# Two-layer cross-attention on one Trainium2 core: the row maxima split on ScalarE and TensorE instead of VectorE, and one 512-column value product per key group

## What is computed

```python
def layer(hidden, context, mask, Wq, bq, Wk, bk, Wv, bv, Wo, bo, gamma, beta):
    q = (hidden @ Wq + bq)      # 8 key groups x 4 heads x 128 x 8
    k, v = context @ Wk + bk, context @ Wv + bv
    scores = einsum('bkgld,bksd->bkgls', q, k) / sqrt(8) + mask
    attn = softmax(scores, axis=-1)
    out = einsum('bkgls,bksd->bkgld', attn, v) @ Wo + bo
    x = out + hidden
    return (x - mean(x)) * rsqrt(var(x) + 1e-6) * gamma + beta
```

## Time and profile before

| | us |
|---|---|
| median of three runs | 337.89 |
| the profiled execution | 340.19 |
| its span on the core | 338.3 |
| TensorE matmul busy | 292.6 (86%) |
| VectorE busy | 271.5 (80%) |
| ScalarE busy | 209.1 (62%) |
| GpSimd busy | 194.0 (57%) |

### The profile page before, as it was taken

The page is one execution under the profiler, slowest core; times in us unless marked ns, Lnnn a source line. Parts: engine busy times, 40 slices in busy tenths (PEclk is TensorE's granted clock), DMA queues, the critical chain, the costliest instruction groups (busy, mean ns, idle before and its releaser), DMA issues.

```text
span 338.3 us, 8301 instructions
## 1 busy us (share of the span) xinstructions
PE 292.6 (86%) x2890; PEld 196.8 (58%) x2890; DVE 271.5 (80%) x625; ACT 209.1 (62%) x500; POOL 194.0 (57%) x335
## 2 busy tenths in 40 slices
PE   7466399599998999999899999999999999888851
PEld 4366276277666776776566666666666666554320
DVE  4426449489988998999899999999999999999441
ACT  3601257277766777777677777777777777656540
POOL 6123305366766776776656666666666666444464
PEclk9756769699999999999999999999999999999795
DMA  7584766714674446344634434444444444420000
GB/s 280 168 237 114 213 182 179 212 31 122 182 242 135 118 124 183 100 125 131 178 101 112 115 109 120 126 121 137 132 119 121 137 141 130 122 64 18 20 16 31
DMA packets 34555, 44.40 MB, mean 131 GB/s; under 512 B 11857, under 2 KB 28241, under 8 KB 31697
## 3 DMA queue, kind: packets, MB, share of 16 engines
q1 hardware_dynamic: 33952, 43.27, 44.7%
q10 hardware_dynamic: 560, 0.59, 0.5%
HBM read 33.10 MB, written 9.96 MB: 127 GB/s over the span
## 4 chain that ended last, share of the span: by engine, by line
PE 37%; DVE 35%; DMA 14%; issue 9%; SPq 2%; ACT 1%; POOL 1%; POOLq 0%; ACTq 0%; DVEq 0%
DVE row_max L460 18%; DMA q_stack<-max_parts 9%; PE misc_bank L663 8%; PE s_bank L567 7%; PE t_bank L587 7%; PE oT_bank L647 7%; DVE o_sb L481 4%; DMA q_scratch<-q_parts 4%; PE qkv_bank L613 3%; DVE z L499 3%; DVE attnT L492 3%; DVE max_parts L468 2%; DVE recip L487 2%; PE qkv_bank L619 2%; PE qkv_bank L623 1%
## 5 line engine op out<-in xcount | busy, mean ns | idle before, releaser
L460 DVE TENSOR_REDUCE row_max<-s_bank 128x4 f32<-128x512 f32 x256 | 168.8, 678 | 35.9 <-PE s_bank L567 35.0
L365 ACT ACTIVATE probs<-t_bank 128x512 f32<-128x512 f32 x256 | 148.0, 601 | 77.8 <-PE t_bank L587 77.4
L587 PE MATMUL t_bank<-q_stack,k_stack 75*128 75x512 bf16 x256 | 99.8, 393 | 20.4 <-DMA q_stack<-max_parts 12.6
L567 PE MATMUL s_bank<-k_stack,q_stack 72*128 72x128 bf16 x1024 | 102.3, 225 | 8.2 <-DMA k_stack<-k_scratch 7.4
L567 PEld LDWEIGHTS s_bank<-k_stack,q_stack 72*128 72x128 bf16 x1024 | 76.2, 101 | 53.1 <-issue 18.5
L307 POOL TENSOR_TENSOR rstd<-var_eps,minus_half 128x1 f32<-128x1 f32 x32 | 17.6, 548 | 56.0 <-DVE var_eps L507 56.0
L316 POOL TENSOR_TENSOR attn<-o_sb,recip 128x256 f32<-128x256 f32 x32 | 20.0, 625 | 40.0 <-DVE recip L487 39.7
L587 PEld LDWEIGHTS t_bank<-q_stack,k_stack 75*128 75x128 bf16 x256 | 25.0, 99 | 28.4 <-ACT probs L365 13.1
L663 PE MATMUL misc_bank<-wo_sb,attnT 128*128 128x256 f32 x128 | 36.0, 405 | 5.7 <-DVE attnT L492 5.7
L190 POOL TENSOR_TENSOR q_rest<-qT,q_parts 128x256 f32<-128x256 f32 x30 | 20.1, 669 | 34.4 <-ACT q_parts L374 34.4
L374 ACT ACTIVATE qT<-qkv_bank,bq_scaled 128x128 f32<-128x128 f32 x60 | 22.1, 369 | 22.6 <-PE qkv_bank L623 20.8
(11 more groups left out here) (76 smaller groups left out, 359.2 us busy)
## 6 DMA issues: line engine op xcount, KB each, us to landing
q_stack<-q_scratch SPq DMA_DIRECT2D x32, 576.0 KB
q_scratch<-q_parts SPq DMA_DIRECT2D x32, 192.0 KB, 6.2
k_stack<-k_scratch SPq DMA_DIRECT2D x32, 144.0 KB
in_sb<-inputs SPq DMA_DIRECT2D x3, 1024.0 KB, 7.9
x_sb<-x SPq DMA_DIRECT2D x4, 512.0 KB, 5.5
result<-y SPq DMA_DIRECT2D x16, 128.0 KB, 1.7
k_scratch<-k_parts SPq DMA_DIRECT2D x48, 32.0 KB, 3.5
mask_sb<-mask SPq DMA_DIRECT2D x1, 1024.0 KB, 7.2
```

The lines of the kernel that those rows point to most:

```text
L365: nc.scalar.activation(probs[:, u % 2, kv], t_bank[kv % 2][:], ACT.Exp).then_inc(exp_done, 1)
L460: nc.vector.tensor_reduce(row_max[:, u % 2, GROUP * kv:GROUP * (kv + 1)], s_bank[(KV * u + kv) % S_BANKS][:].rearrange("p (g s) -> p g s", ...
L567: mm = nc.tensor.matmul(to[:, g * S:(g + 1) * S], q_stack[0:TERM_ROWS, slot, GROUP * kv + g], k_stack[0:TERM_ROWS, slot, kv], start=(g == ...
L587: mm = nc.tensor.matmul(t_bank[kv % 2][:], k_stack[0:STACK_ROWS, slot, kv], q_stack[0:STACK_ROWS, slot, GROUP * kv:GROUP * (kv + 1)], star ...
```

## The change

The three bf16 parts of the maxima are now made without VectorE. ScalarE copies `maxT_ps` as bf16 (part 0). TensorE then adds minus that part onto `maxT_ps` in place, with a product of a 32 x 32 minus identity and the part's rows. ScalarE copies what is left (part 1), TensorE takes it off as well, and ScalarE copies the rest (part 2). `row_max` is transposed one place earlier in the phase, in front of `scores(t, 1)`. ScalarE's `norm` moves behind the third exponential of the phase. In the value product, the two halves now write the same 512 columns: the first half's weights are [v | ones | 0 | 0], the second's [0 | 0 | v | ones], and the second accumulates on the first. So each key group takes one product of 512 columns. The tiles of values get other places for values and zeros, and the rows of Wo are permuted on the host to match. GpSimd makes the minus identity once.

```diff
-MAXT_STEPS, FLIP_STEPS, NORM_STEPS, LN_STEPS = 3, 3, 4, 4
+MAX_PARTS_STEPS, FLIP_STEPS, NORM_STEPS, LN_STEPS = 3, 3, 4, 4
+VHALF = HALF * VW + 2 * HD
...
+        minus_ident = sb("minus_ident", [2 * HEADS, HEADS], BF16)
...
         (SP) load_max_rows
-                sp.wait_ge(maxT_step, MAXT_STEPS * (u + 1))
+                sp.wait_ge(max_part, MAX_PARTS_STEPS * (u + 1))
...
         (ScalarE)
-            def max_first(u):
-                act.wait_ge(maxT_ready, u + 1)
-                need(act, max_rows_loaded[u % 2], 16 * (u // 2))
-                nc.scalar.activation(max_parts[0:HEADS, u % 2], maxT_ps, ACT.Copy).then_inc(max_high, 1)
+            def max_rows(u, part):
+                act.wait_ge(maxT_ready, MAX_PARTS_STEPS * u + part + 1)
+                if part == 0:
+                    need(act, max_rows_loaded[u % 2], 16 * (u // 2))
+                nc.scalar.activation(max_parts[HEADS * part:HEADS * (part + 1), u % 2], maxT_ps,
+                                     ACT.Copy).then_inc(max_part, 1)
...
                 exp(g)
+                if live(t - 1):
+                    max_rows(t - 1, 0)
+                    max_rows(t - 1, 1)
                 exp(g + 1)
                 if live(t - 1):
-                    max_first(t - 1)
+                    max_rows(t - 1, 2)
+                exp(g + 2)
                 if live(t - 4):
                     norm(t - 4)
-                exp(g + 2)
...
         (VectorE)
-            def max_rows(u):
-                high, mid, low = (max_parts[HEADS * n:HEADS * (n + 1), u % 2] for n in range(PARTS))
-                dve.wait_ge(max_high, u + 1)
-                nc.vector.tensor_tensor(mid, maxT_ps, high, ALU.subtract).then_inc(maxT_step, 1)
-                nc.vector.tensor_tensor(rest_ps, maxT_ps, high, ALU.subtract).then_inc(maxT_step, 1)
-                dve.wait_ge(maxT_step, MAXT_STEPS * u + 2)
-                nc.vector.tensor_tensor(low, rest_ps, mid, ALU.subtract).then_inc(maxT_step, 1)
...
         (TensorE)
-                else:
-                    need(pe, maxT_step, MAXT_STEPS * u)
-                nc.tensor.transpose(maxT_ps, row_max[:, u % 2], identf[:]).then_inc(maxT_ready, 1)
+                need(pe, max_part, MAX_PARTS_STEPS * u)
+                nc.tensor.matmul(maxT_ps, row_max[:, u % 2], identf[:], is_transpose=True,
+                                 start=True, stop=False, skip_group_check=True).then_inc(maxT_ready, 1)
+
+            def take_part(u, part):
+                if u == 0:
+                    pe.wait_ge(minus_step, 3)
+                pe.wait_ge(max_part, MAX_PARTS_STEPS * u + part + 1)
+                rows_of = slice(HEADS * part, HEADS * (part + 1))
+                nc.tensor.matmul(maxT_ps, minus_ident[rows_of], max_parts[rows_of, u % 2],
+                                 start=False, stop=(part == 1), skip_group_check=True).then_inc(maxT_ready, 1)
...
-                for odd in range(2):
-                    for j in range(HALF):
-                        kv = half * HALF + j
-                        first = kv * VW + 2 * HD * (1 - odd)
-                        v = v_ones[:, b % RING, first:first + VW] if layer == 0 else v_later[:, b, first:first + VW]
-                        mm = nc.tensor.matmul(
-                            oT_bank[32 * j:32 * (j + 1), half * 2 * L:(half + 1) * 2 * L].rearrange("p (a l) -> p a l", a=2), v,
-                            probs[:, u % 2, kv].rearrange("p (a c l) -> p c a l", a=2, c=2)[:, odd],
-                            start=(odd == 0), stop=(odd == 1), skip_group_check=True)
+                for j in range(HALF):
+                    first = half * HALF * VW + j * VW
+                    v = v_ones[:, b % RING, first:first + VW] if layer == 0 else v_later[:, b, first:first + VW]
+                    mm = nc.tensor.matmul(oT_bank[VW * j:VW * (j + 1)], v, probs[:, u % 2, half * HALF + j],
+                                          start=(half == 0), stop=(half == 1), skip_group_check=True)
...
                 if live(t - 3):
                     probs_v(t - 3, 1)
+                if live(t - 1):
+                    transpose_max(t - 1)
                 scores(t, 1, masked)
                 scoresT(g + 1, masked)
                 if live(t - 1):
-                    transpose_max(t - 1)
+                    take_part(t - 1, 0)
                 scores(t, 2, masked)
                 scoresT(g + 2, masked)
+                if live(t - 1):
+                    take_part(t - 1, 1)
                 if live(t + AHEAD):
                     project(t + AHEAD)
```

More of the change, by code:

```diff
@@ L100, in cross_attention @@
         max_parts = sb("max_parts", [PARTS * HEADS, 2, L], BF16)
[L101 to L102 removed]
+        v_ones = sb("v_ones", [P, RING, 2 * VHALF], F32)
+        v_later = sb("v_later", [P, BATCH, 2 * VHALF], F32)
         probs = sb("probs", [P, 2, KV, GROUP * L], F32)
@@ L172, in cross_attention @@
         maxT_ready = sem("maxT_ready")
-        max_high = sem("max_high")
-        maxT_step = sem("maxT_step")
+        max_part = sem("max_part")
+        minus_step = sem("minus_step")
         scoresT_ready = sem("scoresT_ready")
@@ L206, in blocks_of @@
         def blocks_of(v):
-            return v[:, :, 0:KV * VW].rearrange("p r (h c) -> p r h c", c=VW)
+            return [v[:, :, h * VHALF:h * VHALF + HALF * VW].rearrange("p r (j c) -> p r j c", c=VW) for h in range(2)]
         block = ctx.enter_context(nc.Block())
@@ L295, in _ @@
             nc.gpsimd.memset(mask_sum[:], 0.0).then_inc(sum_cleared, 1)
+            nc.gpsimd.memset(minus_ident[:], 0.0).then_inc(minus_step, 1)
+            for n in range(2):
+                pool.wait_ge(minus_step, n + 1)
+                nc.gpsimd.affine_select(out=minus_ident[:], in_=minus_ident[:], compare_op=ALU.not_equal, fill=-1.0,
+                                        base=-HEADS * n, pattern=[[-1, HEADS]], channel_multiplier=1).then_inc(minus_step, 1)
             nc.gpsimd.memset(minus_half[:], -0.5).then_inc(consts_set, 1)
@@ L298, in _ @@
             pool.wait_ge(v_later_padded, 1)
-            nc.gpsimd.memset(blocks_of(v_later)[:, :, :, 3 * HD:4 * HD], 1.0).then_inc(v_later_padded, 1)
+            for half in blocks_of(v_later):
+                nc.gpsimd.memset(half[:, :, :, HD:2 * HD], 1.0).then_inc(v_later_padded, 1)
             def deviation(u):
@@ L445, in _ @@
             dve.wait_ge(v_padded, 1)
-            nc.vector.memset(blocks_of(v_ones)[:, :, :, 3 * HD:4 * HD], 1.0).then_inc(v_padded, 1)
+            for half in blocks_of(v_ones):
+                nc.vector.memset(half[:, :, :, HD:2 * HD], 1.0).then_inc(v_padded, 1)
             def flag():
@@ L458, in maximum @@
                 if kv == 0:
-                    need(dve, maxT_ready, u - 1)
+                    need(dve, maxT_ready, MAX_PARTS_STEPS * (u - 2) + 1)
                 nc.vector.tensor_reduce(row_max[:, u % 2, GROUP * kv:GROUP * (kv + 1)],
@@ L748 @@
         "w_kv": by_partition(np.concatenate([w[:, k_order] for w in both("Wk")] + both("Wv"), axis=1)),
-        "w_o": np.concatenate([by_partition(w) for w in both("Wo")], axis=1),
+        "w_o": np.concatenate([by_partition(w[o_order]) for w in both("Wo")], axis=1),
         "rows": np.stack([np.concatenate(r) for r in zip(both("bo"), both("gamma"), both("beta"), both("bv"))]),
```

17 lines of the change are left out of this document (7 added, 10 removed).

## The result

On one chip the changed kernel takes 340.96 us (median of four runs, 340.13 to 343.14) and the kernel before 337.92 (four runs, 336.97 to 338.07): a ratio of 1.0106, 95% interval 1.0055 to 1.0156. The forecast was 333.4 and faster, so it is off by 7.6 us and has the wrong sign. The profiled execution of before took 340.19 us (span 338.3), 2.3 above the median that the forecast stood on. The one of after took 341.09 (span 339.0) and lies at its median. So the spans differ by only 0.7, and the forecast for the span, 333.5, was 5.5 us off.

A forecast was written before the change was run, and what follows sets the result against it. TensorE was taken to bound layer 0 and VectorE layer 1; terms of +3.0, -2.0, +0.3, -0.7, -3.2, -2.2 and 0 summed to -4.8 on the 338.3 span, giving 333.4 us, eight in ten between 327.5 and 341.

The forecast's parts named there:

- What bounds the kernel: Whole kernel: TensorE alone sets layer 0's full phases of 8.74 us, VectorE sets layer 1's of 8.48.
- So going in costs 0.09 and coming out 0.10, and one small product costs 0.06 + 0.19 = 0.25.: TensorE's price for each 32 x 32 product, columns plus changes of shape; two make +0.5 us a phase.
- the forecast +3.0: Six full phases of layer 0, each 0.5 us longer by the two small products.
- So they leave 1.5 earlier ... I take -2.0, as the issue moves by more than any of the waits.: Layer 0's four long phases: rows of maxima issued 1.5 us earlier, the wait of 1.09 nearly vanishing, -2.0 together.
- 0 if the landing does not move: Layer 0's four long phases: alternative outcome with no gain, against -2.8 if the wait goes entirely.
- The projections (0.9 or 1.8 us) cover that for TensorE: Each phase: ScalarE's second exponential comes about 0.5 us later, but TensorE does not wait, being busy with projections.
- the 8.12 of layer 1: Nine phases of layer 1: TensorE's 7.62 + 0.5 in place of 8.48, each -0.36, together -3.2 us.
- in place of 8.34: Five phases from 169.0 us: TensorE's 7.84 + 0.5 = 8.34, each -0.14, together -0.7 us.
- the 2.2: Last three phases before 312.5 us: no projection left, VectorE's 0.83 comes out nearly whole, -2.2 us.
- Rival 1: TensorE stands still at the small products in every phase, +0.3 each over 28 phases: slower, 341.5 us; chance 0.22.
- Rival 3: Layer 1 stays at 8.48 through ScalarE's later exponentials or the output projection: 337.0 us, about no change; chance 0.13.
- The step from span to median: Whole kernel: profiled execution 2.3 us above the median, so span forecast 333.5 became 333.1 on the median, given as 333.4.

The follow-up runs named there:

- the full-array run: Changed kernel with both small products over the whole array (weights 96 x 128, zero outside the part) against the kernel before: 339.61 us, ratio 1.0041.
- the value product: Kernel before with only the new value product, one 512-column product per key group, against the kernel before: 338.86 us against 339.55, ratio 1.0001.
- the moves: Kernel before with only the earlier transposition, ScalarE's copy before the second exponential and norm behind the third, VectorE still splitting: 339.69 us, ratio 1.0037.
- its maxima alone: Changed kernel with the old value product, two 256-column products per key group, against the kernel before: 341.26 us, ratio 1.0022.
- its copy with fewer loads: Changed kernel without layer 1's 16 loads of the keys' rows (144 KB each), against the kernel before: 339.93 us against 339.39, ratio 1.0012.
- one product and one subtraction: Layer 0 as before; layer 1 with one whole-array product, two ScalarE copies and one VectorE subtraction, against the kernel before: 334.69 us against 340.25, ratio 0.9873.
- the run with the first part only: Kernel before without VectorE's three subtractions, parts two and three of the maxima zero, against the kernel before: 335.32 us against 339.87, ratio 0.9876.

## Why the prediction was wrong, step by step

**What bounds the kernel.** Right: TensorE in layer 0, VectorE in layer 1. What was not asked is what stands right behind VectorE. The runs found three limits within 0.3 us below 8.48: TensorE with its two products (8.22), ScalarE's way from the transposition to the fifth exponential (8.33), and the transfers of a phase (8.36 on average without the split). The last is no fixed floor, since the changed kernel ran at an even 8.34 with its rows landing 0.3 to 0.9 us before TensorE needed them.

**"So going in costs 0.09 and coming out 0.10, and one small product costs 0.06 + 0.19 = 0.25."** Right to 0.01, and the full-array run showed that 0.09 of it, on the way out, is the change of shape. The neighbour was left out: the float32 products behind the second one cost 0.10 more. A phase of layer 0 pays 0.60, not 0.50. That the full phases still sum to the forecast +3.0 is luck: five paid 0.6 each, and the sixth, 9.31 at a granted clock of 0.94 before and 9.34 at 1.00 after, paid next to nothing.

**"So they leave 1.5 earlier ... I take -2.0, as the issue moves by more than any of the waits."** The step that failed in layer 0, by 2.1 us. The issue did move, by 1.0 to 1.4 us, but the landing moved by -0.1 to +0.2. The prediction had named this case ("0 if the landing does not move") but put -2.0 of -2.8 on the other. The landing follows the transfers ahead of the rows. That is read from the traces, as no run relieved the transfers of layer 0.

**"The projections (0.9 or 1.8 us) cover that for TensorE"** and the 8.12 of layer 1. The failed step of layer 1, 2.1 us. In the changed kernel a phase has 0.10 more for the projections and 0.11 for the exponential that comes late at the seventh product. The late exponential alone would have been enough, since the run over the whole array took the same 8.33 with 0.2 less on TensorE and a wait of 0.32. The same two stand in the phases from 169 us, where 8.56 was measured in place of 8.34 and in place of the 8.48 before, so VectorE's relief gave nothing there (1.1 us). In the last three, which fell by 1.6 of the 2.2, the chain also runs over ScalarE's copies and its second and third exponentials.

**Rival 1** was the right sign by the wrong mechanism, and that its 341.5 lies near the measured 340.96 is luck: TensorE does not stand still at the small products (the wait for the copy is hidden by the drain), and layer 0 pays in the work around them. **Rival 3**, layer 1 does not shorten, came nearest: phases fell by 0.14 instead of 0.36. Of its two causes, ScalarE's later exponentials were the right one; the output projection was not in the way.

**The step from span to median.** I took off 2.3 us because the execution before lay above its median. The one after lay at its median, and so the 0.7 us between the profiles stand against 3.0 between the medians. The phases don't explain the other 2.3. In the profiles of six kernels whose phases are alike to 2 us (before, the value product, the moves, the change, its maxima alone, its copy with fewer loads), the stretch from the eighth transposition to the last takes 206.1 to 207.6 us, while the one ahead of it takes 103.4 to 111.4, without order by kernel. So what the change does to the part behind the eighth transposition is about nothing (206.3 us before, 206.8 after). Whether the 1% of the first comparison lies in the first 106 us for a reason was not found. The two later comparisons of nearly the same code, 1.0022 and 1.0012, have intervals that take in no change, so that the changed kernel is slower rests on the first comparison alone.

## What to carry to other kernels

Before you price the relief of the engine that leads the chain, find the next limits by leaving its work out whole, in a kernel that computes less: here a free relief of VectorE gave 4.2 us, not the 13 that TensorE's slack promised. A step split over engines should go by the slack of each (the nine phases of layer 1 took 73.9 us with one product and one subtraction, 75.1 with two products and 76.1 with three subtractions, each in one profile), and a shape that differs from its neighbours costs in the neighbours too. A transfer that is issued earlier need not land earlier if the transfers ahead of it in its queue did not move.

## What the runs showed that I had not expected

- How long a transfer of 24 KB took hung on how soon it was issued behind the 576 KB load ahead of it. In layer 1 of the kernel before it was issued 6.0 to 6.9 us behind that load and landed 2.8 after its own issue. In the changed kernel it was issued 4.8 to 5.0 behind and took 3.5 to 4.1, and in the run with the first part only it was issued 3.6 to 4.4 behind and took 4.3 to 5.5. So it landed 8.3 to 9.6 us after the load's issue in all three.
- A lone 32 x 32 product of 128 columns took 0.25 us of TensorE's time, and the same product over the whole array with 96 x 128 weights was the cheaper one: 0.07 to its successor instead of 0.16.
- Four float32 products (eight instructions) took 0.99 us behind a small bf16 product, 0.96 behind the same product over the whole array (246.70 to 247.66), and 0.90 behind a 512-column one in the kernel before.
- The round from transposition over ScalarE's copy to the next product took 0.64 us where TensorE waited for it: 0.27 for the transposition, 0.27 for the copy, and 0.05 for each hand-over.
